# Where VectorE's loop of the recurrence begins: at a step's start, or behind the shift of q and k

## The reference

```
xn = layernorm(x)
q, k = silu(causal_dwconv(xn @ Wq)), silu(causal_dwconv(xn @ Wk))   # 4 taps along the tokens
q, k = layernorm of each head's 128 channels, with weight and bias
v, beta, gate = xn @ Wv, sigmoid(xn @ Wb + bb), silu(xn @ Wg)
S_t = (1 - beta_t) * S_(t-1) + beta_t * v_t k_t^T                   # 16 heads, one scan over the tokens
o_t = S_t q_t
s = (o * gate) @ Wo
g = silu(mixture-of-depths FFN(xn))     # top half of each sequence's tokens by score
out = x + s * g
```

## Time and profile before

| | us |
|---|---|
| median of 3 runs | 2673.86 (2671.39 to 2676.84) |
| profiled execution | 2663.39 |
| its span, first to last instruction | 2661.6 |
| busy: PE / DVE / ACT / POOL | 2517.4 / 1813.9 / 1082.2 / 847.6 |
| mean granted TensorE clock | 0.978 of full speed |

### The profile page before, as it was taken

One profiled execution on the slowest core, in us unless ns is written; L12 is line 12 of the kernel. 1 busy time (PEld: TensorE's weight loads), 2 busy tenths in 40 slices (PEclk: granted clock), 3 DMA queues, 4 the chain that ended last, 5 costly groups with the idle time before them and its releaser, 6 DMA issues. The chain is left out here.

```text
span 2661.6 us, 43731 instructions
## 1 busy us (share of the span) xinstructions
PE 2517.4 (95%) x15296; PEld 2224.4 (84%) x15296; DVE 1813.9 (68%) x3332; ACT 1082.2 (41%) x1513; POOL 847.6 (32%) x442
## 2 busy tenths in 40 slices
PE   4899899999999999999999999997899999999997
PEld 4688788889988988889898898997788887888886
DVE  5679899988888988889888898888431212433232
ACT  5444454444434444444444444444432322422221
POOL 2145445434433434334343434344100000121220
PEclk8899999999999999999999999999999999999999
DMA  7555555654445464444456444453471101441320
GB/s 279 175 171 176 167 191 168 221 190 151 162 142 167 158 222 158 143 153 156 152 192 202 151 155 146 158 183 121 153 237 48 58 37 43 136 154 48 110 83 27
DMA packets 232189, 395.55 MB, mean 149 GB/s; under 512 B 58358, under 2 KB 159990, under 8 KB 219130
## 3 DMA queue, kind: packets, MB, share of 16 engines
q1 hardware_dynamic: 125946, 192.21, 22.0%
q10 hardware_dynamic: 97408, 176.71, 19.7%
q0 software_dynamic: 8704, 25.19, 3.1%
HBM read 304.88 MB, written 97.55 MB: 151 GB/s over the span
## 5 line engine op out<-in xcount | busy, mean ns | idle before, releaser
L1008 DVE SCALAR_TENSOR_TENSOR xn_rows<-ps_proj,conv,xn_rows 128x1021 f32<-128x1021 f32 x381 | 486.9, 1278 | 11.6 <-ACT xn_rows L895 2.5
L1185 PE MATMUL ps_proj<-xt_hi,w_hi 128*128 128x512 f32 x1008 | 418.9, 416 | 38.4 <-DVE rc_v_beta L1061 27.4
L1187 PE MATMUL ps_proj<-xt_hi,w_lo 128*128 128x512 f32 x1008 | 403.0, 400 | 0.0
L1186 PE MATMUL ps_proj<-xt_lo,w_hi 128*128 128x512 f32 x1008 | 402.0, 399 | 0.0
L786 POOL TENSOR_TENSOR rc_k_state<-rc_tok_k,k_norm_rows 128x1024 f32<-128x1024 f32 x64 | 153.5, 2399 | 638.5 <-DVE rc_q_silu L1052 554.7
L1207 PE MATMUL ps_proj<-wv_hi,xt_hi 128*128 128x256 f32 x1024 | 295.3, 288 | 0.6 <-PEq L75 0.6
L1208 PE MATMUL ps_proj<-wv_lo,xt_hi 128*128 128x256 f32 x1024 | 289.8, 283 | 0.0
L1209 PE MATMUL ps_proj<-wv_hi,xt_lo 128*128 128x256 f32 x1024 | 289.6, 283 | 0.0
L1185 PEld LDWEIGHTS ps_proj<-xt_hi,w_hi 128*128 128x128 f32 x1008 | 194.2, 193 | 80.4 <-DVE rc_v_beta L1061 29.8
L1187 PEld LDWEIGHTS ps_proj<-xt_hi,w_lo 128*128 128x128 f32 x1008 | 193.5, 192 | 43.9
L1186 PEld LDWEIGHTS ps_proj<-xt_lo,w_hi 128*128 128x128 f32 x1008 | 194.3, 193 | 36.6
(11 more groups left out here) (181 smaller groups left out, 5762.8 us busy)
## 6 DMA issues: line engine op xcount, KB each, us to landing
rc_q_rows<-scratch_q_rows ACTq DMA_DIRECT2D x64, 1024.0 KB
rc_decay_all<-scratch_decay ACTq DMA_DIRECT2D x64, 512.0 KB, 3.7
rc_cum_all<-scratch_cum ACTq DMA_DIRECT2D x64, 512.0 KB, 4.1
scratch_o<-rc_o_sb ACTq DMA_DIRECT2D x64, 512.0 KB, 4.9
w_hi<-scratch_w_split SPq DMA_DIRECT2D x48, 512.0 KB, 4.0
w_lo<-scratch_w_split SPq DMA_DIRECT2D x48, 512.0 KB, 5.2
wv_hi<-scratch_wv_split SPq DMA_DIRECT2D x24, 512.0 KB, 3.9
wv_lo<-scratch_wv_split SPq DMA_DIRECT2D x24, 512.0 KB, 5.0
```

The source lines that it names most:

```text
L1008: nc.vector.scalar_tensor_tensor(out=act_cm[j][:, back:], in0=projected[:, 0:L - back], scalar=conv[par][:, j, t:t + 1], in1=act_cm[j][:, ...
L1185: nc.tensor.matmul(out, hi, xt_hi[:, k, cols], start=k == 0, stop=False)
L1186: nc.tensor.matmul(out, hi, xt_lo[:, k, cols], start=False, stop=False)
L1187: last = nc.tensor.matmul(out, lo, xt_hi[:, k, cols], start=False, stop=k == KC - 1)
```

## The change

VectorE's step is cut in two functions: `first_half` holds everything up to and with `shifts`, `second_half` begins with `convolve(1)` and holds `k_state` and the ranking. `convolve` moves out, with its head and parity as arguments. VectorE no longer uses `steps`; its own loops go over `halves(i)`, which is `second_half` of step i followed by `first_half` of step i+1. The order of VectorE's operations is what it was, and so are its waits; the body still has four second and four first halves. The loops' boundaries lie between `shifts` and `convolve(1)` of an even step. In front of the first loop stand the same peeled steps and one `first_half` more. The other engines' code is not touched.

```diff
-            def step(u, par, odd, split):
+            def convolve(j, A_, par):
...
+            def first_half(u, par, odd):
                 A_, B_, C_, D_ = (At(u, par, lag, odd) for lag in (0, LAG_B, LAG_C, LAG_D))
...
                 if B_.live:
                     shifts()
+
+            def second_half(u, par, odd):
+                A_, C_ = (At(u, par, lag, odd) for lag in (0, LAG_C))
                 if A_.live:
-                    convolve(1)
+                    convolve(1, A_, par)
...
-            steps(dve, step, first_kept_rows)
+            def halves(u, par, odd):
+                second_half(u, par, odd)
+                carry, odd = (0, odd) if par == 0 else (1, 1 - odd)
+                first_half(u + carry, 1 - par, odd)
+
+            first_half(0, 0, 0)
+            for i in range(2 * PEELED_PAIRS):
+                halves(i // 2, i % 2, i // 2 % 2)
+            for first, last in ((PEELED_PAIRS, PPS - 2), (PPS, PAIRS - 2)):
+                with dve.Fori(first, last, 2) as u:
+                    for i in range(4):
+                        halves(u + i // 2, i % 2, i // 2 % 2)
+                for i in range(2 * last, min(2 * last + 4, N - 1)):
+                    halves(i // 2, i % 2, i // 2 % 2)
+            second_half(PAIRS - 1, 1, (PAIRS - 1) % 2)
+            for i in range(N, N + LAG_D):
+                first_half(i // 2, i % 2, i // 2 % 2)
+                second_half(i // 2, i % 2, i // 2 % 2)
+                first_kept_rows(i)
```

More of the change, by code:

```diff
@@ L994, in chunks @@
                 return ap.rearrange("p (c t) -> p c t", t=P)
-            def step(u, par, odd, split):
-                A_, B_, C_, D_ = (At(u, par, lag, odd) for lag in (0, LAG_B, LAG_C, LAG_D))
[L999 to L1010, removed]
+            def convolve(j, A_, par):
+                n = "qk"[j]
+                projected = ps_proj[:, (par + j) % 2]
+                after_step(dve, n + "_tap", A_.i)
+                for t in range(PAD):
+                    back = PAD - t
+                    if t:
+                        after_step(dve, n + "_conv", A_.i, PAD, t)
+                    nc.vector.scalar_tensor_tensor(out=act_cm[j][:, back:], in0=projected[:, 0:L - back],
+                                                   scalar=conv[par][:, j, t:t + 1], in1=act_cm[j][:, back:],
+                                                   op0=ALU.mult, op1=ALU.add).then_inc(S[n + "_conv"], 1)
+            def first_half(u, par, odd):
+                A_, B_, C_, D_ = (At(u, par, lag, odd) for lag in (0, LAG_B, LAG_C, LAG_D))
                 def statistics(j):
@@ L1078, in step @@
                 if A_.live and not first_done(A_.i):
-                    convolve(0)
+                    convolve(0, A_, par)
                 if B_.live:
```

## The result

| | us | ratio to before |
|---|---|---|
| before, median in these runs | 2672.62 (2669.60 to 2676.84) | |
| changed, median | 2627.80 (2625.41 to 2629.53) | 0.9831 [0.9814, 0.9848] |
| changed, run again with other experiments | 2623.98 (2617.75 to 2630.28) | 0.9828 [0.9803, 0.9853] |
| profiled executions, before and changed | 2663.39 and 2628.81 | |

The changed kernel is 44.8 us faster by the medians (2636 was predicted, 2622 to 2656 as the range).

What follows compares the result with a forecast made beforehand. TensorE sets the pace, stalled by VectorE's loop jump, which waits 6.0 us for code fetched anew each iteration. Gains 33 + 0.5 + 5 = 38 us, so 2673.86 - 38 = 2636 us; range 2622 to 2656.

Steps and rivals of the forecast that it cites:

- The jump at 0.2 us, beside 1.17 us of cover: VectorE's jump before k's convolution: 0.2 us if its block is held, hidden in 1.17 us before TensorE's q projection.
- (a): Second loop, nine late VectorE jumps: TensorE gets back 33 us, of idle time and slower clock; 23.4 if clock dips stay.
- the 105.7 that I expected: Second loop after the change: iterations near 105.7 us as a sign that the prediction is right.
- Next late is nothing in the loop: Second loop: with the jump's stall gone nothing else delays TensorE, as one iteration was 105.50 of 106.25 us work.
- (b): The second loop's first jump: TensorE gets back 0.5 us.
- (c): The first loop's one jump: TensorE gets back 5 us, or 0 if GpSimd or VectorE sets the pace there.
- The low end of the range, 2622: Whole kernel: low end of the range said to take the forecast, gain bounds 23 and 39 and run scatter of 5.
- the forecast's own 2630 to 2645: Whole kernel: the jump hits with full gain, 2630 to 2645 us, chance 0.78.
- the first border 15 engine instructions into the old body: VectorE's old loop body: first new code block entered about 15 engine instructions in, then 79 and 85 later.
- Rival 1: VectorE's jump still misses, now in mid-step, q's projection starting 4.8 us late: about 2698 us, chance 0.10.
- its two blocks of 16 KiB, as the prediction read them: VectorE's instruction memory: by the skill's two blocks the jump misses wherever it stands; the prediction took four of 8 KB.

Runs made afterwards that it cites:

- e1: The kernel before with 44 do-nothing semaphore increments ahead of VectorE's first statistics, moving its later code by 44 instructions; 2628.91 us, ratio 0.9841.
- e7: The kernel before with VectorE's code moved by 94 do-nothing instructions; 2628.44 us in its one run.
- e8: The kernel before with VectorE's code moved by 108 do-nothing instructions; 2632.46 us in its one run.
- e9: The kernel before with VectorE's code moved by 33 do-nothing instructions; 2633.23 us, ratio 0.9859.
- e2: The changed kernel with VectorE's code moved by 80 do-nothing instructions; 2655.39 us, ratio 0.9946.
- e11: The changed kernel run again, unaltered, with other experiments; 2623.98 us, ratio 0.9828.
- e12: The changed kernel with VectorE's 64 steps written out without a loop, run again beside the changed kernel; 2625.14 us, ratio 0.9831.
- e6: The kernel before with VectorE's code moved by 32 do-nothing instructions; 2712.22 us in its one run.
- e10: The kernel before with ScalarE's load of the q rows moved behind the store of o; 2761.26 us, ratio 1.0341.
- e3: The changed kernel with VectorE's 64 steps written out, no loop; 2623.05 us, ratio 0.9821.

## Why the prediction was right, and where it was not

**The mechanism is shown, for the position of the code.** Moving the code alone gives the whole gain (e1, e7, e8, e9), moving it back takes most of it (e2), and the flip comes at one instruction (32 and 33). Four blocks held, one of them fetched ahead, is the reading that fits all nine positions of the second loop's four-step body that ran and, counted in the same way, those of the first loops beside them, with packets that come every 128 instructions; what the engine does inside is not seen in any trace.

**The jump at 0.2 us, beside 1.17 us of cover**: 0.3 us, and covered earlier than I had placed it, by the scores.

**(a), nine late jumps, 33 us**: 984.62 - 950.95 = 33.7. The sum is right, its parts were not quite. Seven iterations took 104.93 and not the 105.7 that I expected; the two others 108.97 and 107.44. "Next late is nothing in the loop" is the step that failed: with the jump gone the reload of x is next. It shows at the first of these in TensorE's time order,

```profile
954.02 0.57 PE L1208 MATMUL ps_proj<-xt_hi,w_hi 128*128 128x512 f32 x1 [2.16 <-DMA xt_lo<-scratch_xt_lo]
```

and it costs 108.97 + 107.44 - 2 x 104.93 = 6.5 us. Of these, 4.4 us are TensorE's idle time in the waits above. Before, in the nine iterations of the earlier trace rows, the same two waits came to 0.6 us:

```profile
PE ps_proj L1185 <- DMA xt_lo<-scratch_xt_lo: 0.6, 2, 0.4
```

**(b) and (c)**: the pass with the second loop's first jump went from 106.25 to 105.89, 0.4 us for the 0.5 expected. Its first matmul came at 633.07 in place of 637.50, 4.4 us for the 5 of the first loop. Together 4.4 + 0.4 + 33.7 = 38.5 at the loop's end, for 38 predicted. By the end of the span 34.6 are left; the other 3.9 went behind the loop, where the order of work is the same. From the end of the nine iterations to the end of the span before took 933.2 us and the changed kernel 937.1; the same stretch took 936.3 in the changed kernel's other profile (e11), 933.8 in e12 and 938.2 in e1, so the 3.9 lie within the scatter of single executions. That the medians differ by 44.8 is then a matter of how the profiled execution of before stands to its other runs (2660.14 to 2677.94 in the set of e9 to e12); it stays open why it was that much shorter.

The low end of the range, 2622, does not come out of the terms given for it: 2673.86 - 39 - 5 = 2630, and the measured 2627.80 lies 2 us below that. It is also below the forecast's own 2630 to 2645.

**The position was right by luck of its margin.** I put the first border 15 engine instructions into the old body, from busy times, and took a packet for 79 to 85 of them; counted with the sequencer's instructions it is 33 of 305, and a packet 128. The changed kernel landed in the middle of three blocks by either count (its second loop has 309 instructions, with borders at 115 and 243), but e6 and e8 went wrong by an error of the same kind: they took the border to be at 24.

**Rival 1 was priced too high.** It would have ended at about 2655 (e2), not at 2698: faster than before even with every jump missed. I carried the 6.0 us of the old jump to the new place. There it took 2.9. The stretches show one difference between the two jumps, before's first, from branch to next instruction (length, busy times, clock, DMA share, GB/s):

```profile
855.20:861.20 6.00, 4.93 (x26) 3.94 (x24) 0.14 (x2) 4.10 (x4) 1.06 (x1) 1.00 0.87 263
```

and e2's:

```profile
877.44:880.30 2.86, 2.86 (x26) 2.85 (x26) 0.91 (x2) 0.24 (x1) 0.00 (x0) 1.00 0.01 3
```

The old jump fetches while the DMA engines are 87% busy at 263 GB/s, mostly with the 1 MB of q rows issued 0.6 us earlier; the new one while they are idle. The code packet begins 4.2 us after the branch before and 1.0 us after it in e2, and from there to the next instruction it is 1.8 us in both: the difference lies wholly ahead of the packet.

The trace of before holds the comparison that e10 missed. At the first of the second loop's ten jumps ScalarE issued the load of the q rows 0.6 us behind VectorE's branch, and the jump took 3.2 us at the same place of the same loop; at the other nine the load went out 0.4 to 1.4 us ahead of the branch, and they took 5.7 to 6.3 us. The first jump's instructions and its stretch:

```profile
L648 DVEq COMPARE_BRANCH  x1: 56/56/56, 639.2 to 639.2; - x1
...
L648 DVEq FUSED_REGOPS  x1: 57/57/57, 642.4 to 642.4; - x1
...
L919 ACTq DMA_DIRECT2D rc_q_rows<-scratch_q_rows x1: 339/339/339, 639.8 to 639.8; - x1
...
639.22:642.40 3.18, 3.18 (x15) 2.63 (x14) 0.11 (x1) 1.03 (x1) 1.06 (x1) 1.00 0.68 180
```

So the start of a step does not by itself make a miss dear. Busy DMA engines alone don't either: the first loop's missed jump in e9, 4.5 us behind such a load, took 3.9 us at a DMA share of 1.04 and 352 GB/s.

```profile
302.34:306.24 3.90, 3.83 (x22) 3.04 (x20) 0.13 (x2) 3.60 (x4) 1.06 (x1) 1.00 1.04 352
```

That the fetch queues behind a load issued just ahead of it fits these rows, but it rests on one jump without the load and is not shown. It is not the only cause either: the first loops' jumps in before and e2 took 5.9 and 5.6 us with no such load in the 4 us ahead of the branch. There a border lies 6 and 4 instructions ahead of the jump, so the useless fetch may stand in the way of the needed one; that wasn't tried.

The Trainium skill, "Runtime: NRT & Kernel Launch", section "Instruction fetch mechanics", has the stall on a branch to code that is gone, and the runs agree with that (0.3 us with the code there, 2.9 to 6.0 without). By its two blocks of 16 KiB, as the prediction read them, the changed kernel would miss too; it doesn't, and VectorE's packets are of 8 KB.

## What to carry to other kernels

Where a loop's body is about as long as the code that an engine holds, look at two things in the profile before anything else: how many instruction packets one iteration brings, and how long after the branch the engine's next instruction starts. If packets come in every iteration, the position of the body decides as much as its length; a few do-nothing instructions ahead of the loop (e1) and no loop at all (e3) were equal cures here; fewer steps in the body should be a third, but no run tried it. Any later edit ahead of the loop can undo the first (e2). After such a gain read the waits again: here the reload of x, once hidden behind the jump, is the next 6 us.

## What the runs showed that was not expected

- A jump whose target is the last instruction of a block, as I read it, waits twice: 5.9 us, and then until 8.96 us of idle time had passed (e6, 2712.22 against 2674.22 before).
- The same miss costs 2.9 us with idle DMA engines, 6.0 us where a load of 1 MB was issued just ahead of the branch, and 3.2 us where it was issued just behind; VectorE's 64 steps without any loop fetch all their code unseen (e3).
